# The blend stage of a two-layer graph network: 192 columns of the layer normalization by ScalarE, 64 by VectorE

## The reference

```python
x = _layernorm(x + _L0_gnn_ref(x, edge_index, W, att_src, att_dst, bias, skip_W))
x = _layernorm(x + _L1_gnn_ref(x, edge_attr_8, edge_attr_4, ..., edge_index))

# _layernorm, rows of 256:   (x - mean) / sqrt(var + 1e-05)
# the end of _L0_gnn_ref:    elu(agg / (denom + EPS) + bias + x @ skip_W)
```

## Time and profile before

| what | us |
|---|---|
| median of 3 runs | 6061.02 (6052.65 to 6061.88) |
| the profiled execution | 6073.1 |
| its span, first to last instruction | 6071.4 |
| stage A and what is ahead of it | 0 to about 2340 |
| blend stage | about 2340 to 2635 |
| stage C | about 2635 to 5785 |
| stage D | from about 5785 |

### The profile page before, as it was taken

How to read it: one execution, slowest core, us unless ns; L and a number is a source line. 1 busy time by engine, 2 the same in 40 slices (tenths; PEclk the granted TensorE clock), 3 DMA queues, 4 the chain that set the end, 5 groups by cost and what they waited for, 6 DMA issues and landing times.

```text
span 6071.4 us, 211848 instructions
## 1 busy us (share of the span) xinstructions
PE 5657.3 (93%) x41086; PEld 4550.0 (75%) x41087; DVE 5431.3 (89%) x17528; ACT 3457.0 (57%) x12685; POOL 4647.0 (77%) x3868
## 2 busy tenths in 40 slices
PE   7899999999999997789999999999999999999876
PEld 5455555555555555579999999999999999999765
DVE  2899999999999998989999999999999999999777
ACT  2566666666666665655555555555555555555466
POOL 2777777777777774458888888888888888888877
PEclk9899999999999999999999999999999999999999
DMA  6799999999999996469999999999999999999997
GB/s 202 216 269 267 268 269 267 266 268 267 266 267 267 266 268 182 136 148 178 178 178 178 178 177 177 178 175 176 178 176 177 178 177 176 176 177 175 155 278 229
DMA packets 1269411, 1272.43 MB, mean 210 GB/s; under 512 B 220911, under 2 KB 1205744, under 8 KB 1269264
## 3 DMA queue, kind: packets, MB, share of 16 engines
q0 software_dynamic: 328176, 468.28, 46.2%
q1 hardware_dynamic: 941186, 803.62, 45.7%
HBM read 682.35 MB, written 588.89 MB: 209 GB/s over the span
## 4 chain that ended last, share of the span: by engine, by line
PE 52%; DMA 14%; issue 11%; DVE 9%; SPq 4%; DVEq 4%; ACT 3%; POOL 2%; ACTq 0%; POOLq 0%
DMA part<-arena,c_idx 13%; PE PS L905 10%; PE PS L1008 9%; PE PS L990 8%; PE PS L895 6%; PE PS L979 6%; PE PS L1023 6%; PE PS L1006 4%; SPq L437 2%; DVE big L1279 2%; DVEq L362 2%; POOL part L603 2%; DVE big L1217 1%; PE PS L846 1%; DVE big L1225 1%
## 5 line engine op out<-in xcount | busy, mean ns | idle before, releaser
L603 POOL DMA_INDIRECT part<-arena,c_idx x1664 | 2596.6, 1560 | 530.2 <-issue 341.5
L574 POOL DMA_INDIRECT big<-h_tab,big x1664 | 1631.6, 981 | 526.0 <-issue 364.4
L905 PE MATMUL PS<-big 128*128 128x260 f32 x3328 | 972.5, 411 | 155.6 <-DVE big L1217 148.6
L1008 PE MATMUL PS<-w2m,arena 128*128 128x128 f32 x6656 | 1103.7, 288 | 0.0
L905 PEld LDWEIGHTS PS<-big 128*128 128x128 f32 x3328 | 556.1, 189 | 443.4 <-issue 333.1
L1008 PEld LDWEIGHTS PS<-w2m,arena 128*128 128x128 f32 x6656 | 876.9, 192 | 0.0
L990 PE MATMUL PS<-arena 128*128 128x256 f32 x3328 | 860.7, 381 | 15.3 <-ACT arena L781 14.8
L1225 DVE TENSOR_TENSOR big<-big,PS 128x260 f32 x1664 | 700.0, 421 | 168.7 <-PE PS L905 118.5
L678 ACT ACTIVATE big<-PS,arena 128x128 f32<-128x128 f32 x1664 | 513.3, 359 | 502.7 <-PE PS L895 501.4
L780 ACT COPY arena<-PS 128x512 f32<-128x512 f32 x832 | 488.8, 588 | 545.0 <-DMA part<-arena,c_idx 493.3
L757 ACT COPY arena<-PS 128x384 f32<-128x384 f32 x1664 | 719.2, 487 | 28.4 <-PE PS L979 3.0
(11 more groups left out here) (194 smaller groups left out, 10950.0 us busy)
## 6 DMA issues: line engine op xcount, KB each, us to landing
w_tab<-big SPq DMA_DIRECT2D x416, 520.0 KB
arena<-w_tab SPq DMA_DIRECT2D x1664, 130.0 KB
part<-arena SPq DMA_DIRECT2D x1664, 32.1 KB
ot_tab<-big SPq DMA_DIRECT2D x416, 128.0 KB
arena<-ot_tab SPq DMA_DIRECT2D x416, 128.0 KB
arena<-src_tab SPq DMA_DIRECT2D x416, 128.0 KB
big<-part SPq DMA_DIRECT2D x392, 128.5 KB, 3.0
big<-h_tab,big POOLq DMA_INDIRECT x1664
```

The costliest lines, as they stand in the source:

```text
L574: pool.indirect_dma_start(hg[:, s, k, :], None, h_tab, bass.IndirectOffsetOnAxis(ap=sidx[:, s, k:k + 1], axis=0)).then_inc(s_hg[s], 16)
L603: pool.indirect_dma_start(part[q], bass.IndirectOffsetOnAxis(ap=c_idx[:, s, k:k + 1], axis=0), o_cmb[:, s, k, :], None, compute_op=ALU.add ...
L905: mm(PS[:, 2 + k % 2, 0:HW], oh[:, p, k, :], hg[:, p, k, :], start=True, stop=True).then_inc(s_agg, 1)
L1008: last = mm(o_v[:, k, 2 * j:2 * j + 2, :].rearrange("p j u -> p (j u)"), midT[:, k, 1 + j, :], w2m[:, (1 + 2 * j) * MUL:(3 + 2 * j) * MUL] ...
```

## The change

In the blend stage the 192 columns leave VectorE. ScalarE computes them as one activation, `scale * x + offset`, where the scale is the reciprocal standard deviation of the row and the offset is -mean times it. VectorE computes that offset in a new instruction on one column, which goes to column 2 of `mv`, and signals `s_bnm`; ScalarE signals `s_bxv`. VectorE's wait for GpSimd's result (`s_brstd`) moves with the new instruction to the head of its step; the 64 columns stay where they were. ScalarE's new instruction stands at the head of its step. TensorE's transposes and SyncE's store wait for both parts.

```diff
@@ -324,9 +324,9 @@
         slots = "0 1 2 3"
         s_ownin, s_ownp, s_own = sems("a_own", "in p sum")
         s_hg, s_otst, s_ea, s_sh, s_wst = (sems(f"a_{n}", slots) for n in ("hg", "otst", "ea", "sh", "wst"))
-        (s_rden, s_bsum, s_bskip, s_bv, s_bm, s_be, s_belu, s_bs, s_bmv, s_brstd, s_bx1, s_bxp, s_bxT, s_by,
+        (s_rden, s_bsum, s_bskip, s_bv, s_bm, s_be, s_belu, s_bs, s_bmv, s_brstd, s_bx1, s_bxv, s_bnm, s_bxp, s_bxT, s_by,
          s_bout, s_br, s_bmid, s_blo) = sems(
-            "b", "rden sum skip v m e elu s mv rstd x1 xp xT y out r mid lo")
+            "b", "rden sum skip v m e elu s mv rstd x1 xv nm xp xT y out r mid lo")
         s_bin, s_bst = sems("b_in", slots), sems("b_st", slots)
         (s_cy, s_csh, s_csame, s_cix, s_cpr, s_cmid, s_ccnt, s_cnum, s_cmt, s_cmT, s_co, s_cos, s_cov, s_cturn, s_csum, s_ccmb) = sems(
             "c", "y sh same ix pr mid cnt num mt mT o os ov turn sum cmb")
@@ -467,7 +467,8 @@
                     sp.dma_start(b_xT[:, n, :, :], xv[:, :, ds((b + 3) * P, P)]).then_inc(s_bin[n], 16)
                 m = (s - 2) % TURN
                 if there(b - 2):
-                    wait(sp, s_bx1, 2 * (b - 1))
+                    wait(sp, s_bx1, b - 1)
+                    wait(sp, s_bxv, b - 1)
                     sp.dma_start(one(x1b, b - 2), b_x1[:, m, :]).then_inc(s_bst[m], 16)
 
             steps(sp, NB, 3, 2, step_b)
@@ -722,6 +723,12 @@
                 def y_part(block, i):
                     return y3[:, ds(block, 1), i, :].rearrange("p o d -> p (o d)")
 
+                if there(b - 1):
+                    wait(act, s_bnm, b)
+                    wait(act, s_bst[m], landed(b - 5, m) if there(b - 5) else 0)
+                    a.activation(b_x1[:, m, MUL:D].rearrange("p (d u) -> p d u", d=3),
+                                 b_v[:, m, MUL:D].rearrange("p (u d) -> p d u", d=3), ACT.Identity, bias=mv[:, m, 2:3],
+                                 scale=mv[:, m, 3:4]).then_inc(s_bxv, 1)
                 if there(b - 3):
                     wait(act, s_by, b - 2)
                     a.copy(y_part(b - 3, 0), PS[:, Y_MAP_BANK[n % 2], 0:D]).then_inc(s_bout, 1)
@@ -958,7 +965,8 @@
                     mm(PS[:, SKIP_BANK[n % 2], 0:D], b_xT[:, n, 1, :], skw[:, 1, :], start=False, stop=False)
                     mm(PS[:, SKIP_BANK[n % 2], 0:D], ones[:, :], brow[:, :], start=False, stop=True).then_inc(s_bskip, 1)
                 if there(b - 1):
-                    wait(pe, s_bx1, 2 * b)
+                    wait(pe, s_bx1, b)
+                    wait(pe, s_bxv, b)
                     wait(pe, s_bxT, b - 1)
                     for j in range(2):
                         last = nc.tensor.transpose(PS[:, B_T_BANK, j * P:(j + 1) * P], b_x1[:, m, j * P:(j + 1) * P], ident[:, :])
@@ -1308,6 +1316,10 @@
 
             def step_b(b, s, there):
                 n, m = (s + 1) % TURN, (s - 1) % TURN
+                if there(b - 1):
+                    wait(dve, s_brstd, b)
+                    v.scalar_tensor_tensor(mv[:, m, 2:3], mv[:, m, 0:1], -1.0, mv[:, m, 3:4], ALU.mult, ALU.mult
+                                           ).then_inc(s_bnm, 1)
                 if there(b + 1):
                     v.tensor_tensor(b_v[:, n, :].rearrange("p (h c) -> p h c", h=H),
                                     acc[:, ds(b + 1, 1), 0:D].rearrange("p o (h c) -> p (o h) c", h=H),
@@ -1328,15 +1340,11 @@
                     v.scalar_tensor_tensor(b_v[:, s, :], b_v[:, s, :], 0.0, b_e[:, s, :], ALU.max, ALU.add
                                            ).then_inc(s_bs, 1)
                 if there(b - 1):
-                    wait(dve, s_brstd, b)
                     wait(dve, s_bst[m], landed(b - 5, m) if there(b - 5) else 0)
                     normalized(b_x1[:, m, 0:MUL], b_v[:, m, 0:MUL], m).then_inc(s_bx1, 1)
                 if there(b):
                     wait(dve, s_bs, b + 1)
                     v.bn_stats(stat[:, s, :], b_v[:, s, :]).then_inc(s_bmv, 1)
-                if there(b - 1):
-                    normalized(b_x1[:, m, MUL:D].rearrange("p (d u) -> p d u", d=3),
-                               b_v[:, m, MUL:D].rearrange("p (u d) -> p d u", d=3), m).then_inc(s_bx1, 1)
                 if there(b):
                     mean_and_variance(s, b, s_bmv)
                 if there(b - 3):
```

## The result

| kernel | median us | runs | ratio to before |
|---|---|---|---|
| before | 6060.5 | 4 (6052.7 to 6061.9) | |
| the change | 6149.9 | 4 (6145.6 to 6160.4) | 1.0148, 95% interval 1.0135 to 1.016 |

The change costs 89 us, where 87 were forecast: 6149.9 against 6148. The profiled execution took 6146.2 us with a span of 6144.5. The sum came out; one of its two terms did so for another reason than the one given, and the experiments are mostly about that.

A forecast was written before the change was run, and what follows sets the result against it. VectorE was taken to set the blend stage's pace. The new period with its pause (+49 us) and the collision with GpSimd's subtraction (+38) sum to +87 us on the 6061.0 median: 6148 us, range 6098 to 6163.

The forecast's parts named there:

- The removal gives 0.23 us, not 0.51: VectorE's row: taking away the 192 columns saves 0.23 us a block, since half their time covered a bn_stats dependency.
- The product costs 0.08: Head of VectorE's step: the new 128x1 product keeps the next instruction off for 0.08 us.
- The pause of 0.81: VectorE ahead of the product: the wait for GpSimd's reciprocal root lies bare, 0.81 us from addition to product each block.
- The loop's turn: VectorE, every fourth block: the turn's 0.30 us falls inside the pause and is saved.
- The block at 3.39 us without collision, +49 us: VectorE's blend period: 3.39 us against 2.88, +0.51 a block, +49 us over 97 steps.
- The collision in each block, +38 us: GpSimd's subtraction goes ahead of VectorE's 64 columns in 93 blocks, 0.41 us each, +38 us; chance 0.60.
- the disturbed block of the earlier trace: Block in the profile before where GpSimd's subtraction starts 0.02 us behind the 64 columns, which take 0.74 instead of 0.31.
- The margin of 0.01 us: Computed start of GpSimd's subtraction behind VectorE's 64 columns in the changed kernel, 1.43 against 1.42 us after the product's start.
- ScalarE's instruction: ScalarE's new 192-column activation, head of its step: 0.63 us long, next start after 0.47, from the nearest stage D row.
- The pause alone: Rival, blend stage: 64 columns get in ahead of GpSimd's subtraction, no collision, +49 us, 6110 us; chance 0.29.
- Faster through a hidden wait: Rival, VectorE: no standing still, row of 2.65 us, -0.15 over 97 steps, 6046 us; chance 0.05.
- TensorE's granted clock: Rival, blend stage: clock falls to the lower level, +0.6 us a block more, up to 6205 us; chance 0.02.

The follow-up runs named there:

- e1: Kernel before, with only the 128x1 product and its wait at the head of VectorE's step, all 256 columns staying on VectorE: +117 us, ratio 1.0155 to 1.019.
- e3: The change with the blend stage written out as straight code on all engines, no loop: +81 us over the kernel before, ratio 1.0097 to 1.0132.
- e2: The change with VectorE's product directly ahead of the 64 columns and ScalarE's activation behind the two bf16 copies: +38 us over before, ratio 1.0036 to 1.007.
- e6: The change with its loop, only ScalarE's 192 columns moved behind the two bf16 copies: +115 us over the kernel before, ratio 1.0156 to 1.0189.
- e4: As e3, with ScalarE's 192 columns also moved behind the two bf16 copies: +105 us over the kernel before, ratio 1.0135 to 1.0169.
- e5: Kernel before with its blend stage written out as straight code, no loop: +38 us over the kernel before, ratio 1.0037 to 1.0071.
- e12: The change in straight code, product late, bn_stats covered, GpSimd's subtraction held back, ScalarE reordered, TensorE's transposes a step later: 6038.5 us, 0.9937 to 0.9964 of before.
- e10: Kernel before in straight code, GpSimd's subtraction also waiting for VectorE's 64 columns: -7 us against the kernel before, ratio 0.9983 to 1.0002.

## Why the prediction was right, and where it was not

**The removal gives 0.23 us, not 0.51.** Right: bn_stats to bn_aggr is 0.52 or 0.53 after (2499.97 to 2500.50). In the loop even the 0.23 was nearly all lost again behind it. In e1, where the 192 columns still stand there, bn_stats to the addition of epsilon takes 0.77 + 0.09 + 0.31 = 1.17 us; in the change it takes 0.53 + 0.26 + 0.34 = 1.13 on average. The 0.51 us of work taken off VectorE shortened its row by some 0.04.

**The product costs 0.08.** Right in straight code (0.08 in e3), 0.25 in the loop. See below.

**The pause of 0.81.** Right to a hundredth, L589 at 0.55 included, and shown by e1 (the product and its wait alone lose as much as the whole change) and by e2 against e6 (the product moved back, and nothing else, regains 92 us). The loop's turn does fall inside it: L1324 comes 0.25 or 0.26 behind the product in all four slots.

**The block at 3.39 us without collision, +49 us.** Right as a sum: the blocks of e3 without collision take 3.41.

**The collision in each block, +38 us.** This step failed. The mechanism exists, at about the price given (0.47 us a block in e3, 3.88 against 3.41), and it decides blocks in straight code, but the change pays it in four blocks only, some 2 us, and the kernel before paid it in four as well. The step that misled me is where I read the earlier trace rows: in an ordinary block L584 starts 0.28 us after ScalarE's copy, and I took that for the lock, L584 waiting for L1306. e3 shows that a GpSimd instruction which loses the lock starts on time and takes longer. The 0.28 is what the start of this instruction takes in the loop. It is 0.27 to 0.30 in at least 87 blocks of 98 in each of the seven kernels with the loop, whatever VectorE runs beside it, and 0.08 in at least 95 blocks of 98 in e3, e4 and e5. I carried the 0.07 of the earlier trace rows into the loop. By the rows above, with 0.08 L585 would have started at 2499.71, 0.04 ahead of L1314, and collided. That the disturbed block of the earlier trace rows was one of those written out ahead of the loop was in the code, and e5 confirms that this was all that set it apart. The margin of 0.01 us that made me hesitate was none: e5's blocks, nearly all with GpSimd 0.01 to 0.03 behind, all collide. ScalarE's instruction was mis-sized too: the next one starts 0.55 us behind it, not 0.47. In straight code that brings GpSimd from the computed 0.01 to 0.06 or 0.07 behind the 64 columns, the very edge, and so only half of e3's blocks collide.

**What took its place.** In the loop's blocks the product's follower comes 0.17 us later than computed, L1353 0.12 to 0.23 later (0.17 on average) and L1311 0.03 later: 0.37 us a block over some 88 blocks, 33 us. With 49 us for the pause and 2 for four collisions these make 84 us, against 83 measured in the stage. The prediction had no term for this at all. e3 shows that the gaps go with the loop, 0.08 and 0.10 us in place of 0.25 and 0.21 to 0.32. What in the loop's code makes them was not tested. It has address and wait instructions between the work (the two `ISA` rows behind the product in the order of the program, and two waits ahead of L1353 in the source), and my reading is that they are dealt with ahead of time while VectorE's row is full and not behind a wait that really ends late.

So 6148 against 6149.9 is better than the working deserves: a term of 38 us with the wrong cause stood in for one of 33 us that I had left out. A late start of the same kind may be what before shows at each loop turn, 0.30 us; I counted that only as something saved.

**The rivals.** The pause alone, at +49, had no place for the dispatch and is 34 us short in the stage. Faster through a hidden wait did not happen, as VectorE's idle time shows. TensorE's granted clock was 0.98 in the stretch from 2400 to 2670 shown above, with TensorE busy 166 of 270 us, so the change did not bring it to the lower level.

## What to carry to other kernels

Before work is taken off the busiest engine, look at what the piece covers: here its 0.51 us hid a dependency behind bn_stats, and the edit also moved a wait from behind four long instructions (L1312, L1320, L1325 and L1328: four, not the three named with the change) to directly behind its own cause. The instruction that hands something to another engine should be as far as possible from the one that takes the answer back; moving the same product behind the four instructions was worth 92 us in the stage (e6 to e2). A change that takes work off an engine is judged against the kernel before with the same repairs: e12 is 31 us shorter in the stage than before, and 21 of them remain against e10. When an engine begins to wait, the order of its neighbours shifts by tenths of a microsecond, and pairs on VectorE and GpSimd that missed each other can meet: a wait that pins GpSimd's start to a harmless place was worth 0.44 us a block in straight code (e5 to e10).

## What the runs showed of the hardware

- VectorE and GpSimd exclude each other on more than one form. The instruction of VectorE that lost took 0.66 to 0.79 in place of 0.31 (tensor_scalar, 64 columns), up to 0.93 in place of 0.42 (two tiles in SBUF; 0.92 in e4) and 0.62 in place of 0.15 (the 128x1 product, e2). Other forms ran beside GpSimd's subtraction, which reads SBUF too, without such a loss: bn_stats 0.41 to 0.47, tensor_tensor with one input in PSUM 0.39 to 0.44, and the 192 columns read with a step of three 0.50 to 0.56, in all the overlaps of these runs.
- The loser can be told by its duration: L589 0.77 in place of 0.67 where VectorE was first (e3). The Trainium skill's page "SBUF — State Buffer" (SBUF: two separate sides) says that the shared port pair goes to the one that starts first, for its whole instruction. By the starts in the trace that holds for the forms with two tiles in SBUF: where GpSimd's subtraction started 0.03 to 0.3 us ahead they took 0.65 to 0.93 (L1324 in e6), and where it started together with them or behind they took 0.41 to 0.43. It does not hold for the 64 columns: VectorE's record starts first and GpSimd still goes ahead when it starts up to 0.06 us behind, either of the two at 0.07, and VectorE from 0.08 on. I take it that this form claims the port some 0.07 us after its record starts; no run tests that by itself.
- The same GpSimd subtraction starts 0.08 us after the copy that it waits for in straight code and 0.28 us after it in a loop (e3, e4 and e5 against the kernels with the loop). Behind a wait that ended late VectorE's next instruction shows the like: 0.08 us behind the product in straight code, 0.25 in the loop.
- ScalarE's 192 columns with a step of three, scale and offset from columns, take 0.64 us and hold the next back by 0.55, where the nearest row, with the step in what is written, had 0.63 and 0.47. The prediction's estimate of 0.53 us is 0.11 short.
